# Attention over 32 heads: the loops of four engines written out as straight code with constant waits

## What is computed

```python
x = L0_attn_x                                   # (2, 2048, 256) float32
mod = (silu(c) @ wmod).reshape(2, 6, 1, 256)    # shifts, scales and gates
h = layernorm(x) * (1 + ca) + sa
x = x + ga * attention(h)                       # 16 heads of 16, LoRA on q, k, v, o
h = layernorm(x) * (1 + cb) + sb
x = x + gb * ffn(h)                             # shared SwiGLU + top-1 of 8 experts

# attention, for each of 2 * 16 = 32 pairs of batch and head:
energy = einsum('nqhd,nkhd->nhqk', Q, K) / sqrt(16)    # 2048 x 2048 per head
attn = softmax(energy, axis=-1)
out = einsum('nhqk,nkhd->nqhd', attn, V)
```

## Time and profile before

| | us |
|---|---|
| median of 3 runs | 2066.53 |
| lowest, highest | 2063.53, 2069.93 |
| the profiled execution | 2066.09 |
| its span | 2064.5 |
| PE busy | 1900.7 (92%) |
| DVE busy | 1581.8 (77%) |
| ACT busy | 1180.4 (57%) |

### The profile page before, as it was taken

One profiled execution on the slowest core, in us unless ns is written; L12 is line 12 of the kernel. 1 busy time (PEld: TensorE's weight loads), 2 busy tenths in 40 slices (PEclk: granted clock), 3 DMA queues, 4 the chain that ended last, 5 costly groups with the idle time before them and its releaser, 6 DMA issues.

```text
span 2064.5 us, 39255 instructions
## 1 busy us (share of the span) xinstructions
PE 1900.7 (92%) x12334; PEld 707.0 (34%) x12335; DVE 1581.8 (77%) x2802; ACT 1180.4 (57%) x1354; POOL 321.3 (16%) x361
## 2 busy tenths in 40 slices
PE   8688999989999899998999989999994799999997
PEld 5332222222222222222222222222213556566664
DVE  5377998989999899898999989989925832244443
ACT  5444776767777677776777767767781221111111
POOL 6544000000000000000000000000005722223332
PEclk9898999999999999999999999999997899999999
DMA  4540111111112111121111211111027532322221
GB/s 163 156 144 27 40 41 53 58 41 40 40 42 67 43 40 40 40 69 45 40 40 38 67 47 37 38 37 63 17 62 245 194 103 92 112 78 69 69 69 46
DMA packets 89774, 142.00 MB, mean 69 GB/s; under 512 B 13104, under 2 KB 60208, under 8 KB 89472
## 3 DMA queue, kind: packets, MB, share of 16 engines
q1 hardware_dynamic: 74336, 102.01, 15.8%
q0 software_dynamic: 10240, 32.40, 4.9%
q10 hardware_dynamic: 5024, 5.24, 0.7%
HBM read 90.84 MB, written 48.51 MB: 67 GB/s over the span
## 4 chain that ended last, share of the span: by engine, by line
PE 82%; issue 5%; DVE 5%; DMA 3%; POOL 2%; ACT 1%; SPq 1%; DVEq 0%; POOLq 0%; ACTq 0%
PE ps L857 24%; PE ps L846 20%; PE ps L812 15%; PE ps L1529 7%; PE ps L1080 5%; PE ps L1547 3%; PE ps L1413 3%; DVE mx L916 2%; DMA l_in<-inverse_sums 2%; PE ps L552 1%; ACT prob L960 1%; POOL parts L693 1%; PE ps L1538 1%; POOL rest L689 1%; PE ps L561 1%
## 5 line engine op out<-in xcount | busy, mean ns | idle before, releaser
L916 DVE TENSOR_REDUCE mx<-ps 128x1 f32<-128x512 f32 x2048 | 1278.0, 683 | 115.8 <-PE ps L812 85.0
L960 ACT ACTIVATE prob<-ps 128x1024 f32<-128x1024 f32 x1024 | 993.5, 1021 | 360.3 <-PE ps L846 357.9
L857 PE MATMUL ps<-prob,vs 128*32 128x512 f32 x4096 | 555.8, 615 | 0.6 <-ACT prob L960 0.6
L812 PE MATMUL ps<-k_high,q_high 64*128 64x512 bf16 x2048 | 416.1, 391 | 52.1 <-DVE mx L916 34.9
L846 PE MATMUL ps<-q_high,k_high 64*128 64x512 bf16 x2048 | 392.7, 380 | 31.1 <-issue 28.4
L846 PE MATMUL ps<-q_low,k_low 34*128 34x512 bf16 x2048 | 393.1, 380 | 0.0
L812 PEld LDWEIGHTS ps<-k_high,q_high 64*128 64x128 bf16 x2048 | 101.6, 93 | 696.9 <-DVE mx L916 640.4
L990 POOL COPY vs<-v_all 128x256 f32 (+1 forms) x32 | 12.7, 400 | 1206.0 <-PE ps L857 1206.0
L846 PEld LDWEIGHTS ps<-q_high,k_high 64*128 64x128 bf16 x2048 | 101.7, 96 | 117.9 <-issue 34.7
L846 PEld LDWEIGHTS ps<-q_low,k_low 34*128 34x128 bf16 x2048 | 100.5, 95 | 116.6 <-issue 2.3
L1578 ACT ACTIVATE esig<-ps 128x512 f32<-128x512 f32 x39 | 23.3, 597 | 195.9 <-PE ps L1529 195.9
(11 more groups left out here) (145 smaller groups left out, 1317.0 us busy)
## 6 DMA issues: line engine op xcount, KB each, us to landing
k_high<-qk_parts SPq DMA_DIRECT2D x128, 128.0 KB
qk_parts<-parts SPq DMA_DIRECT2D x32, 384.0 KB, 3.7
q_high<-qk_parts SPq DMA_DIRECT2D x128, 64.0 KB
k_low<-qk_parts SPq DMA_DIRECT2D x128, 64.0 KB
head_out<-head_out_sb SPq DMA_DIRECT2D x32, 256.0 KB, 10.7
sorted_in<-zero_row POOLq DMA_DIRECT2D x13, 390.0 KB, 7.2
xs<-sorted_in SPq DMA_DIRECT2D x39, 130.0 KB
q_low<-qk_parts SPq DMA_DIRECT2D x128, 32.0 KB
```

The source lines that it names most:

```text
L812: pe.matmul(ps[:, ring_bank(2 * m + u), :], q_high[p][mine, t * P:(t + 1) * P], k_high[p][mine, c * CH:(c + 1) * CH], start=True, stop=Tru ...
L857: mm = pe.matmul(ps[32 * j:32 * j + 32, 7, :], vs[buf(h)][:, kt, :], prob[:, kt % 2, j * CH:(j + 1) * CH], start=(kt == 0), stop=(kt == KT ...
L916: dve.tensor_reduce(mx[:, at, c:c + 1], ps[:, ring_bank(k), :], AX.X, ALU.max).then_inc(s_ring, 1)
L960: act.activation(prob[:, kt % 2, :].rearrange("p (u c n) -> p u c n", u=2, c=2)[:, :, half, :], ps[:, 2 * half:2 * half + 2, :], ACT.Exp). ...
```

## The change

The loops over the heads on SP, PE, DVE and ACT are replaced by Python loops, which write every head out. The number of a head is then a constant, all waits compare with constants, and no branch, no loop index and no register instruction is left in these four streams between the first and the last head. Order and operands of the engine instructions are the same. POOL's loop and all loops of the other stages stay.

```diff
@@ attend_sync
-            trips = (NH - 5) // NB
-            with sp.Fori(0, trips) as i:
-                for u in range(NB):
-                    turn((i, 1 + u), 2)
-            for n in range(1 + NB * trips, NH):
+            for n in range(1, NH):
                 turn((0, n), NH - 1 - n)
@@ attend_tensor
-            with pe.Fori(0, (NH - 2) // NB) as i:
-                for u in range(NB):
-                    turn((i, u), 2)
-            turn((0, NH - 2), 1)
-            turn((0, NH - 1), 0)
+            for n in range(NH):
+                turn((0, n), min(NH - 1 - n, 2))
@@ attend_vector
-            with dve.Fori(0, (NH - 2) // NB) as i:
-                step.turns(i, NB)
-                for u in range(NB):
-                    head((i, 1 + u))
-            step.close((NH - 2) // NB, NB)
-            for n in range(1 + (NH - 2) // NB * NB, NH - 1):
-                head((0, n))
-            head((0, NH - 1), last=True)
+            for n in range(1, NH):
+                head((0, n), last=n == NH - 1)
@@ attend_scalar
-            for kt in range(KT):
-                exps(0, kt)
-            with act.Fori(1, NH) as n:
+            for n in range(NH):
                 for kt in range(KT):
                     exps(n, kt)
-                    if kt == 0:
+                    if n and kt == 0:
                         head_copy(n - 1)
```

## The result

| | before | after |
|---|---|---|
| median, us | 2065.72 (4 runs, 2063.53 to 2069.93) | 1998.26 (4 runs, 1996.05 to 2001.02) |
| ratio | | 0.9672, 95% interval 0.9651 to 0.9693 |
| span of the profiled execution | 2064.5 | 1999.3 |
| head 1 to head 31, `mneg` to `mneg` | 1294.34 | 1226.76 |

A forecast was written before the change was run, and what follows sets the result against it. DVE's reductions were taken to bound an ordinary head at 40.89 us. 2066.09 - 67.6 for PE's and DVE's branches, all other terms 0, gave 1998.5; the median being 0.4 above, the forecast was 1999 us, range 1994 to 2008.

The forecast's parts named there:

- The bound and the loss: Heads 1 to 31: DVE's reductions limit an ordinary head at 40.89 us; removing PE's and DVE's branches saves 67.6 us.
- What one trip costs: PE's and DVE's branches back: gaps of 2.5 and about 3.5 us plus some of 2.2 for clock, 6 to 8.2.
- Constants in place of registers: Register instructions and waits in the 30 heads: removing them gains 0, bounds 0 and -11.7 us.
- ACT: ACT's loop over heads: its branch is hidden by 9.9 us of slack per head, so writing it out gains 0.
- that rival: ACT's written-out stream stalls at each new code block: up to 43 us lost, time up to 2041, chance 0.05.
- The term for head 31: Head 31, where PE and ACT set the pace: constant waits gain between 0 and -2.2 us, taken as 0.
- SP: SP's loads and `mb` copies: shorter issue gains nothing and a stall of a few us costs nothing, so 0.
- The instruction queues: Instruction packets over the span: q8 from 112 to about 95, q14 from 62 to less than 40.
- The gaps are not the branches': Something else every three heads, such as POOL's large transfer, makes the gaps: nothing gained, 2066 us, chance 0.02.
- The clock falls in the unbroken stretch: PE, working some 1290 us without rest, is granted 1.2 GHz for long: slower, 2103 us for 96 steps, chance 0.03.
- The Trainium skill's figure for a compare-and-branch: At about 108 ns, 18 branches and ACT's 30 would be worth 5.2 us, time 2060.9; the prediction decided against it.

The follow-up runs named there:

- The loop of one trip: The changed kernel with 30 heads of PE and 30 of DVE each put in a single-trip loop, no branch back taken: 1997.49 us, 0.9633 of before.
- PE's loop alone: The changed kernel with PE's loop of ten trips put back, DVE, ACT and SP still written out: 2043.23 us, 0.9862 of before.
- DVE's loop alone: The changed kernel with DVE's loop of ten trips put back, PE, ACT and SP still written out: 2033.07 us, 0.981 of before.
- that loop begun a head later: The changed kernel with PE's loop as before and DVE's loop of nine trips starting at head 2: 2064.9 us, 0.9982 of before.

## Why the prediction was right, point by point

**The bound and the loss.** The step that carried the prediction was the count: 30 heads in 1294.34 us against 30 ordinary heads of 40.89, and the missing 67.6 us found as nine gaps on each of two engines. The stage lost 1294.34 - 1226.76 = 67.6 us. The single heads of the changed kernel are all at 40.9, and so are the 21 of the kernel before that hold no branch. This part was read and counted, not lucky.

**What one trip costs.** The total per trip was right, its parts were sketched too evenly. A DVE branch alone costs 2.1 or about 3.6 us, a PE branch 3.3 to about 6, by whether the lower clock follows. I had added a gap of 2.5, a gap of 3.5 and up to 2.2 for the clock, once for both. The rows for these parts were of the first trip, which isn't a typical one: its head took 50.77 us, and the slow step of the earlier trace rows lies behind DVE's gap, where later trips kept the full clock. By themselves the two loops cost 32.4 and 43.7, together 67.6, not 76.1: with both loops the clock fell behind PE's gap in all nine trips, behind DVE's only in the first two.

**Constants in place of registers.** Taken as 0, with -11.7 as an end. The heads without a branch measured it: 40.89 us with registers and with constants. The loop of one trip, meant for this, held no register instructions.

**ACT.** The branch was worth nothing, as said, and its stream written out brought no stall at a new block, so that rival falls: with ACT written out no head is above 40.9. The term for head 31 was mis-sized, in its sign too: I bounded it between 0 and -2.2 us, by ACT's idle time, and took 0; it was +0.7. I had looked for what constants remove and not at where the built code puts two waits on one instruction.

**SP.** Worth nothing, as said.

**The instruction queues.** q8 went from 112 packets to 89, where I said about 95: 23 packets for nine branches are 2.6 each and not one to two. It is back at 112 with PE's loop alone and stays at 89 with DVE's loop alone, so q8 is PE's. q14 went from 62 to 45, where I said less than 40. The step that failed is that q14 is DVE's alone. With ACT's and SP's loops put back it had 30, with them written out 45: it carries other engines' blocks too, and so its rows bore on ACT's fetches as well.

**The rivals.** "The gaps are not the branches'" falls with the changed kernel itself and the loop of one trip, where POOL's loop is the same and no gap is left. "The clock falls in the unbroken stretch" falls with the 1.00 over 1227 us. The Trainium skill's figure for a compare-and-branch (Advanced Engine Details and Errata, control flow timing, about 108 ns) is not what a branch costs here once its body is long. The Trainium skill's rule in Runtime: NRT & Kernel Launch, section on instruction fetch mechanics, that a taken branch out of the window stalls, agrees in kind with the runs: long bodies stall, short ones don't. Its size doesn't: the same section puts what an engine other than PE holds at 512 instructions, and here bodies of 407 on DVE and 415 on ACT, both shorter, stalled in every trip.

## What to carry to other kernels

Before costing a loop, count ordinary trips against the stage's length and look for "issue" gaps as many as there are branches back: on PE and DVE, with bodies of some 2100 and 407 instructions, each branch here was a gap of 2.2 to 3.5 us, and PE's lower clock could follow it. (Two branches of a longer body took 4.6.) The engine that sets the pace, and the one that feeds it, are the ones to write out (a loop of one trip did the same); on engines with slack the loop may stay and keeps the code short. Constants in the waits were worth nothing here beside reductions of 0.68 us, and of two waits ahead of one instruction the one that ends last belongs on the instruction itself.

## What the runs showed of the hardware that I had not expected

The price of the same branch varies: PE's gap was 2.7 to 3.5 us with one block on the instruction queue and 4.6 with two. A gap of about 2 us on PE is followed by a stretch at 1.2 GHz in some cases and not in others: behind all nine branches with DVE's loop alone, behind three of eight with that loop begun a head later, behind two of nine in the kernel before; and two of PE's own gaps, of 3.2 and 3.4 us, were not followed by one. A loop body on ACT of some 250 instructions repeats without a stall that shows, where one of 415 stalls; 0.8 us of that stall shows, and by the queue's blocks it may have been about 2. And a loop of one trip was built with constants in its waits, so it can't serve to test registers.
